# Attention plus mixture of experts on one core: the last stage unrolled, with twelve pairs of gathered rows, eight sums and eight residual rows in flight

## What is computed

```python
xn = layernorm(x)                                  # x: 2 x 2048 x 512, float32
out = x + attn(xn) + ffn(xn)
# attn: 16 heads of 32, latent keys and values of 128, causal softmax; out projection Wo, bias bo
# ffn: 8 experts, the two with the highest gate logit of each token
all_out = relu(einsum('nsd,edo->nseo', x, expert_w) + expert_b)
ffn = take_along_axis(all_out, top_idx).mean(axis=2)
```

## Time and profile before

| What | Value |
|---|---|
| Median of 3 timed runs | 1820.98 us |
| The profiled execution's own time | 1818.49 us |
| Its span, from the first to the last instruction | 1816.8 us |
| PE busy | 1619.3 us (89%) |
| DVE, ACT, POOL busy | 1207.6, 987.9, 583.0 us |
| Mean granted clock of TensorE, as a share of full speed | 0.963 |

### The profile page before, as it was taken

One profiled execution on the slowest core, in us unless ns is written; L12 is line 12 of the kernel. 1 busy time (PEld: TensorE's weight loads), 2 busy tenths in 40 slices (PEclk: granted clock), 3 DMA queues, 4 the chain that ended last, 5 costly groups with the idle time before them and its releaser, 6 DMA issues.

```text
span 1816.8 us, 46170 instructions
## 1 busy us (share of the span) xinstructions
PE 1619.3 (89%) x13286; PEld 919.7 (51%) x13287; DVE 1207.6 (66%) x2682; ACT 987.9 (54%) x1884; POOL 583.0 (32%) x972
## 2 busy tenths in 40 slices
PE   4676675988999999999999999999999899998776
PEld 2566662444555555555555555555555355554332
DVE  3888877556777777777777777777777244444555
ACT  2556661555666666666666666666666533333332
POOL 1456652566212112112112112211211333332554
PEclk8898996999999999999999999999999899999999
DMA  5486764011001001001001001101100155555776
GB/s 142 136 248 197 239 186 114 21 29 24 24 24 47 23 23 47 23 23 47 24 23 42 28 23 37 33 23 31 39 23 24 47 173 173 173 173 151 229 233 220
DMA packets 126985, 160.87 MB, mean 89 GB/s; under 512 B 28352, under 2 KB 77504, under 8 KB 126816
## 3 DMA queue, kind: packets, MB, share of 16 engines
q1 hardware_dynamic: 108336, 121.15, 21.9%
q0 software_dynamic: 12992, 35.77, 7.2%
q10 hardware_dynamic: 5616, 3.45, 0.6%
HBM read 99.03 MB, written 61.15 MB: 88 GB/s over the span
## 4 chain that ended last, share of the span: by engine, by line
PE 73%; DVE 10%; DMA 5%; issue 5%; ACT 4%; POOL 1%; ACTq 1%; DVEq 0%; SPq 0%; another core or an unknown queue 0%; POOLq 0%
PE PS L1209 28%; PE PS L1156 26%; PE PS L1259 10%; DMA arena<-expert_rows,cur 4%; PE PS L1221 3%; DVE pm L967 3%; PE PS L1242 2%; ACT arena L671 1%; ACT arena L683 1%; PE PS L1127 1%; DVE arena L1030 1%; PE PS L1104 1%; DVE arena L841 1%; PE PS L1110 1%; DMA eb_bc<-in_expert_b 1%
## 5 line engine op out<-in xcount | busy, mean ns | idle before, releaser
L967 DVE TENSOR_REDUCE pm<-PS 128x1 f32<-128x512 f32 (+3 forms) x1280 | 731.5, 602 | 301.9 <-PE PS L1156 287.9
L712 ACT ACTIVATE arena<-PS 128x512 f32<-128x512 f32 (+1 forms) x1152 | 607.9, 575 | 281.2 <-PE PS L1156 266.8
L1156 PE MATMUL PS<-arena 96*64 96x512 f16 (+7 forms) x5120 | 726.1, 355 | 38.0 <-DVE pm L967 20.2
L1209 PE MATMUL PS<-arena 128*33 128x512 f32 (+3 forms) x2560 | 661.9, 534 | 1.0 <-POOL arena L541 1.0
L1156 PEld LDWEIGHTS PS<-arena 96*64 96x64 f16 (+1 forms) x5120 | 353.2, 110 | 369.3 <-issue 143.3
L541 POOL TENSOR_SCALAR_AFFINE_SELECT arena<-arena 128x256 f32<-128x256 f32 (+1 forms) x256 | 110.9, 433 | 406.7 <-ACT arena L712 403.3
L1209 PEld LDWEIGHTS PS<-arena 128*33 128x33 f32 x2560 | 172.8, 112 | 85.4 <-POOL arena L541 3.6
L1156 PE MATMUL PS<-later,deny 128*64 128x128 f16 x1024 | 173.6, 222 | 0.0
L1259 PE MATMUL PS<-w_hi,arena 128*128 x576 | 172.1, 381 | 0.3 <-issue 0.3
L729 ACT ACTIVATE arena<-PS 128x1024 f16<-128x1024 f32 x72 | 73.8, 1024 | 150.5 <-PE PS L1242 145.1
L1007 DVE SCALAR_TENSOR_TENSOR arena<-PS,eb_bc 128x512 f32<-128x512 f32 x72 | 49.8, 691 | 127.0 <-PE PS L1259 127.0
(11 more groups left out here) (172 smaller groups left out, 1643.5 us busy)
## 6 DMA issues: line engine op xcount, KB each, us to landing
expert_rows<-arena SPq DMA_DIRECT2D x72, 256.0 KB, 2.0
arena<-q_pieces SPq DMA_DIRECT2D x96, 128.0 KB
arena<-k_pieces SPq DMA_DIRECT2D x96, 128.0 KB
v_rows<-arena SPq DMA_DIRECT2D x8, 1056.0 KB, 7.0
arena<-v_rows SPq DMA_DIRECT2D x32, 264.0 KB
arena<-in_x SPq DMA_DIRECT2D x8, 1024.0 KB, 7.1
xn_rows<-arena SPq DMA_DIRECT2D x16, 512.0 KB, 4.6
arena<-in_expert_w SPq DMA_DIRECT2D x32, 256.0 KB, 4.0
```

Source lines behind the costliest of these rows:

```text
L712: a.activation(probs[kk % 4][:, a_ * CH:a_ * CH + w], PS[:, s2_bank(k, x), 0:w], ACT.Exp, scale=SCALE).then_inc(s["exp_done"], 1)
L967: v.reduce_max(pm[:, c, r, p:p + 1], PS[:, S1_BANK[n], 0:w], AX).then_inc(s["s1_done"], 1)
L1156: last = t.matmul(PS[h:h + P // 2, bank, cols], lhsT[:, h:h + P // 2], rhs, start=start, stop=stop)
L1209: last = t.matmul(PS[rows_, 6 + c % 2, CH - wds[a]:CH], v_sb[pu % 2][:, j + a, :], probs[pk % 4][:, a * off:a * off + wds[a]], start=p_ in ...
```

## The change

- The two buffers each of gathered pairs, sums and residual rows become rings of 12, 8 and 8. The gathered rows and the sums lie where `w_hi` and `w_lo` were; the experts' last matmul has read them before POOL passes its wait for all 72 stores. The residual rows take the room in arena2, and `x_g`'s three further buffers have their own places there.
- Every buffer of the rings has a semaphore of its own, which starts at zero.
- SP waits for `norm_done` after the attention stage and loads the first eight residual rows before it stores the first tile of the experts. In the last stage it stores the sum of tile n and then loads the residual row of tile n + 8.
- POOL no longer copies indices to `cur`: each gather reads its column of `place` directly. It waits for the sum of tile n - 12 from tile 12 on.
- DVE waits for the store of tile n - 8, PE for the first instruction of the sum of tile n - 2 (the one that reads PSUM) in place of its last.
- On all engines the stage's loop over pairs is written out: 32 tiles, with constants in place of register values. The order of the operations on ACT, DVE and PE is as before.

```diff
-        xc = [tD(E) for _ in range(B)]
...
-        acc = [tD(E) for _ in range(B)]
-        y_g = [[tD(E) for _ in range(TOP)] for _ in range(B)]
-        x_g = [x_g0[:, :]] + [y_g[q // 2][q % 2].bitcast(f16) for q in range(1, AHEAD_G)]
+        x_ahead = [tD(E).bitcast(f16) for _ in range(AHEAD_G - 1)]
+        xc = [tD(E) for _ in range(8)]
+        spare = [w[:, :, :].rearrange("p e f -> p (e f)").bitcast(f32)[:, q * E:(q + 1) * E]
+                 for w in (w_hi, w_lo) for q in range(NE * KB * E // (2 * E))]
+        y_g, acc = [spare[TOP * q:TOP * (q + 1)] for q in range(12)], spare[TOP * 12:]
+        x_g = [x_g0[:, :]] + x_ahead
...
@@ SyncE @@
+            sp.wait_ge(s["norm_done"], count(NC * BH))
+            for n in range(len(xc)):
+                residual(n)
             with sp.Fori(0, PT // 2) as i:
                 for u in range(2):
                     sp.wait_ge(s["y_done"], count(i * 2 + u + 1))
                     sp.dma_start(y_dram[ds((i * 2 + u) * P, P), :], y_sb[u]).then_inc(s[f"y_st{u}"], 16)
-            for u in range(B):
-                residual(0, u)
-            with sp.Fori(0, ST - 1) as i:
-                for u in range(B):
-                    result(i, u)
-                    residual(i + 1, u)
...
+            for n in range(NT):
+                result(n)
+                if n + len(xc) < NT:
+                    residual(n + len(xc))
...
@@ GpSimd @@
-            with pool.Fori(0, ST) as i:
-                for u in range(B):
-                    n = i * B + u
-                    pool.wait_ge(s["acc_done"], count(n - 1))
-                    g.tensor_copy(cur[:, TOP * u:TOP * (u + 1)],
-                                  place[:, :, ds(i + u * ST, 1)].rearrange("p k o -> p (k o)")).then_inc(s["cur_done"], 1)
-                    pool.wait_ge(s["cur_done"], count(PT + n + 1))
-                    pool.sem_inc(s["gather_at"], 1)
-                    for k in range(TOP):
-                        g.indirect_dma_start(out=y_g[u][k], out_offset=None, in_=y_dram,
-                                             in_offset=bass.IndirectOffsetOnAxis(ap=cur[:, TOP * u + k:TOP * u + k + 1], axis=0)
-                                             ).then_inc(s[f"yg_in{u}"], 16)
+            for n in range(NT):
+                q, at = n % len(y_g), n // B + n % B * ST
+                if n >= len(y_g):
+                    pool.wait_ge(s["acc_done"], count(n - len(y_g) + 1))
+                for k in range(TOP):
+                    g.indirect_dma_start(out=y_g[q][k], out_offset=None, in_=y_dram,
+                                         in_offset=bass.IndirectOffsetOnAxis(ap=place[:, k, at:at + 1], axis=0)
+                                         ).then_inc(s[f"yg_in{q}"], 16)
...
@@ VectorE @@
-                dve.wait_ge(s[f"out_done{u}"], count(i * 16))
-                dve.wait_ge(s[f"xc_in{u}"], count((i + 1) * 16))
+                if n >= len(acc):
+                    dve.wait_ge(s[f"out_done{r}"], n // len(acc) * 16)
+                dve.wait_ge(s[f"xc_in{x_}"], (n // len(xc) + 1) * 16)
                 dve.wait_ge(s["proj_ps"], count(n + 1))
...
-                dve.wait_ge(s[f"yg_in{u}"], (i + 1) * (16 * TOP))
...
+                dve.wait_ge(s[f"yg_in{y_}"], (n // len(y_g) + 1) * (16 * TOP))
...
@@ TensorE @@
-                    pe.wait_ge(s["acc_done"], count(n - 1))
+                if n >= B:
+                    pe.wait_ge(s["dveE"], count((n - B) * 2 + 1))
```

More of the change, by code:

```diff
@@ L214, in layer_kernel @@
         START = 4
[L215 to L216 removed]
+        FROM_ZERO = ["id_zero", "id_done", "ids_in", "xg_in0", "xg_in1", "xg_in2", "xg_in3"] + OUT_SEMS
         def count(n):
@@ L444, in _ @@
                     sp.dma_start(y_dram[ds((i * 2 + u) * P, P), :], y_sb[u]).then_inc(s[f"y_st{u}"], 16)
[L446 to L451, removed]
-            for u in range(B):
-                residual(0, u)
-            with sp.Fori(0, ST - 1) as i:
-                for u in range(B):
-                    result(i, u)
-                    residual(i + 1, u)
-            for u in range(B):
-                result(ST - 1, u)
-            for w in range(B):
-                sp.wait_ge(s[f"out_done{w}"], count(16 * ST))
+            for n in range(NT):
+                result(n)
+                if n + len(xc) < NT:
+                    residual(n + len(xc))
+            for q in range(len(acc)):
+                sp.wait_ge(s[f"out_done{q}"], 16 * len(range(q, NT, len(acc))))
         @block.gpsimd
@@ L748, in turned_heads @@
                              PS[:, 4 + 2 * u:6 + 2 * u, :].rearrange("p z c -> p (z c)"), ACT.Copy).then_inc(s["oT_done"], 1)
-            for u in range(B):
-                first_piece(0, u)
-            with act.Fori(0, ST - 1) as i:
-                for u in range(B):
-                    turned_heads(i * B + u, u)
-                    first_piece(i + 1, u)
-            for u in range(B):
-                turned_heads((ST - 1) * B + u, u)
+            for n in range(B):
+                first_piece(n)
+            for n in range(NT):
+                turned_heads(n)
+                if n + B < NT:
+                    first_piece(n + B)
         @block.vector
@@ L1027, in sums @@
                 dve.wait_ge(s["proj_ps"], count(n + 1))
-                lnk(v.scalar_tensor_tensor(out=acc[u], in0=PS[:, u, :], scalar=1.0 / WS, in1=xc[u], op0=ALU.mult, op1=ALU.add))
-                dve.wait_ge(s[f"yg_in{u}"], (i + 1) * (16 * TOP))
-                lnk(v.tensor_tensor(acc[u], acc[u], y_g[u][0], ALU.add))
-                v.tensor_tensor(acc[u], acc[u], y_g[u][1], ALU.add).then_inc(s["acc_done"], 1)
-            for u in range(B):
-                second_piece(0, u)
-            with dve.Fori(0, ST - 1) as i:
-                for u in range(B):
-                    second_piece(i + 1, u)
-                    sums(i, u)
@@ L1039, in _ @@
-            for u in range(B):
-                sums(ST - 1, u)
+                lnk(v.scalar_tensor_tensor(out=acc[r], in0=PS[:, u, :], scalar=1.0 / WS, in1=xc[x_], op0=ALU.mult, op1=ALU.add))
+                dve.wait_ge(s[f"yg_in{y_}"], (n // len(y_g) + 1) * (16 * TOP))
+                lnk(v.tensor_tensor(acc[r], acc[r], y_g[y_][0], ALU.add))
+                v.tensor_tensor(acc[r], acc[r], y_g[y_][1], ALU.add).then_inc(s["acc_done"], 1)
+            for n in range(B):
+                second_piece(n)
@@ L1043, in _ @@
+            for n in range(NT):
+                if n + B < NT:
+                    second_piece(n + B)
+                sums(n)
         @block.tensor
@@ L1280, in turn_heads @@
                 last.then_inc(s["otp_ps"], 1)
-            def outs(i, more):
-                for u in range(B):
-                    n = i * B + u
-                    if u == 0 or more:
-                        turn_heads(n + 1, 1 - u)
-                    pe.wait_ge(s["oT_done"], count(n + 1))
-                    pe.wait_ge(s["acc_done"], count(n - 1))
-                    terms = [(k, z, y) for k in range(KB) for z, y in pairs]
-                    for q_, (k, z, y) in enumerate(terms):
-                        last = t.matmul(PS[:, u, :], oT[u][:, z, k, :], comb_hl[:, y, k, :],
-                                        start=q_ == 0, stop=q_ == len(terms) - 1)
-                    last.then_inc(s["proj_ps"], 1)
-            turn_heads(0, 0)
-            with pe.Fori(0, ST - 1) as i:
-                outs(i, True)
-            outs(ST - 1, False)
+            turn_heads(0, 0)
+            for n in range(NT):
+                u = n % B
+                if n + 1 < NT:
+                    turn_heads(n + 1, 1 - u)
+                pe.wait_ge(s["oT_done"], count(n + 1))
+                if n >= B:
+                    pe.wait_ge(s["dveE"], count((n - B) * 2 + 1))
+                terms = [(k, z, y) for k in range(KB) for z, y in pairs]
+                for q_, (k, z, y) in enumerate(terms):
+                    last = t.matmul(PS[:, u, :], oT[u][:, z, k, :], comb_hl[:, y, k, :],
+                                    start=q_ == 0, stop=q_ == len(terms) - 1)
+                last.then_inc(s["proj_ps"], 1)
 _INS = ["x", "Wq", "Wdkv", "Wuk", "Wuv", "ln_g", "ln_b", "Wo_h", "Wo", "bo", "gate_w", "gate_b", "expert_w", "expert_b"]
```

32 lines of the change are left out of this document (19 added, 13 removed).

## The result

The changed kernel took 1810.34 us (median of 6 runs, 1803.05 to 1812.82) beside 1819.78 us for the kernel before (6 runs). The ratio is 0.9942, with a 95% interval of 0.9921 to 0.9962: faster by 0.58%, 9.4 us, where 42.7 us were forecast. The profiled execution's span is 1808.4 us, 8.4 less than before.

The account below looks back on a forecast made before the run. The prediction took the last stage to be bound by a chain of waits for gathered rows, 9.18 us a pair of tiles. Terms -45.2 + 1.5 + 1.0 = -42.7 us from 1820.98 gave 1778.3, rounded to 1778.0; range 1772 to 1790.

Parts of the forecast that it names:

- At no cost: Last stage: PE's earlier wait, semaphores, constants and written-out code cost nothing; the range holds 9.6 us for POOL's gaps.
- POOL's port: Rival, last stage: gathers beside DVE's two-input instructions take 1.62 us each, 4.8 us more, 1783 in all; chance 0.18.
- PE's pace: Last stage: with rows ready, the loop of PE and DVE sets 3.06 us a tile, where a tile took 4.59.
- The late first rows: Start of the last stage: the first tile's sum waits for its gathered rows, 1.6 us once.
- The gathers: Last stage: POOL's two gathers per tile take 2.92 us, just under PE's 3.06; late landings are charged 1.5 us.
- The sign that I had named: Last stage, if right: gathers 1.25 to 1.6 us apart up to tile 12, then held by the sum.
- The last stage as a whole: Last stage: 45.2 us gained by the faster pace, less 1.5 us for late landings of gathered rows.
- The residual rows at the start: Start of the expert stage: eight residual loads delay the first awaited gathers by 1.0 us, bounds 0 and 6.0.
- The sum: Whole kernel: -45.2 + 1.5 + 1.0 = -42.7 us.
- DMA as a bound: Rival, last stage: transfers need 3.34 us a tile, more than PE's 3.06, so 1781 to 1791 us; chance 0.22.
- the share at 1.0 that I had named as its sign: Last stage: DMA share at 1.0, waits for residual or gathered rows throughout and landings over 5 us would show DMA bounding.
- The full exclusion of gathers and two-input instructions: Rival, last stage: gathers and DVE's two-input instructions take turns, 4.69 us a tile against 4.59, 1825 in all; chance 0.03.

Follow-up runs that it names:

- the later runs: The changed kernel, unedited, timed again on four occasions on three chips beside the kernel before: 37 to 44 us gained.
- changed_again: The changed kernel without an edit, run once more beside the kernel before: ratio 0.9777.
- loops8: The changed kernel with the last stage's loops back on ACT, PE and DVE and 8 gathered pairs instead of 12: 1758.09 us beside 1797.87, ratio 0.9785.
- lead4: The changed kernel with POOL waiting for the sum of tile n - 4 instead of n - 12: 1757.20 us beside 1797.87, ratio 0.9783.
- rings2: The changed kernel with rings of two; written-out code, removed index copy and PE's earlier wait stay: 1778.64 us beside 1797.87, ratio 0.9891.

## Why the prediction was wrong, and where it was right

**What failed in the measured case.** The step that failed is "At no cost", which put semaphores and written-out code at nothing, with a range that held 9.6 us for what the rows had no price for. It took for granted that a signal of PE reaches ACT and DVE at once beside a stream of gathers. The rival "POOL's port" looked for the gathers' disturbance in DVE's port only. In the first measurement PE's signals came up to 29 us late, and the last stage took 31 us more for it (137.4 against 106.6 us). That the rest of the sum holds in the later runs leaves this step as the one that made the forecast miss. The kernel before had a trace of it that I didn't read: from 330 to 450 us, where PE did 817 matmuls, it has waits of DVE and ACT marked "issue" and "remote". I had looked only at the stages that the change touches.

**What held.** Set against the later runs, where the conditions of that measurement are absent, the working comes out term by term, with one term too small:
- PE's pace. Forecast 3.06 us a tile. In `changed_again`, from PE's turn at 1652.30 (tile 2) to 1742.93 (tile 31) are 29 steps of 3.125 us on the average, with the early delays in it.
- The late first rows. Forecast 1.6 us once. Measured there: four short waits for rows at the start, 1.8 us in all, and PE's waits for L1014 of 3.4 us in three (2.4 of them stand before the stage's first turn in both kernels).
- The gathers. Forecast 1.25 to 1.62 us each, 1.46 taken. Measured 1649.03 to 1734.8 for 63 steps: 1.36. Landings were later than I took, 5.3 us in the median (3.2 to 6.9) instead of 3.85, but after the first tiles they are covered. POOL never waited for a sum, so the ring of twelve never filled. The sign that I had named, gathers held by the sum from tile 12 on, didn't come, and four pairs are enough.
- The last stage as a whole. Forecast 45.2 - 1.5 = 43.7 us shorter. Measured 151.0 us from PE's first turn in the profile before (1816.8 - 1665.8) and 106.6 in `changed_again`, 44.4 shorter. A profile of the kernel before in the later conditions isn't on record; its last stage has none of the waits in question.
- The residual rows at the start. Forecast 1.0 us, between 0 and 6.0. Measured 12.61 - 9.09 = 3.5 us (3.1 in the first measurement). This term was too small by 2.5 us: I argued that different queues share at once. In `changed_again` PE starts on the two first gathers 5.9 and 7.1 us after their issue (1413.77 to 1419.66, 1415.86 to 1422.98), where 3.6 us were before:

```profile
1415.86 0.98 POOL L594 DMA_INDIRECT arena<-xn_rows,cur_id  x1 [0.84 <-POOL cur_id L591]
...
1422.98 1.03 PE L1236 MATMUL PS<-ident,arena 128*128 128x128 f16 x8 [2.30 <-DMA arena<-xn_rows,cur_id]
```

- The sum. -42.7 us forecast; -41.1, -37.5, -44.0 and -40.2 us on the four occasions.

**The rivals.** DMA as a bound: its share is 1.00 in `changed_again` at 362 GB/s and PE still has no wait for it, so the share at 1.0 that I had named as its sign isn't one. The overlap of packets that the earlier trace rows showed fits this. The full exclusion of gathers and two-input instructions, at the price that I gave it, didn't come: in the stretch from 1653.79 to 1664.95 the gathers take 0.96 to 1.29 us beside DVE. But they do take turns, for a short part of the gather. Two pairs of rows show the two cases:

```profile
1700.71 0.76 DVE L1026 TENSOR_TENSOR w_lo<-w_lo,w_hi 128x512 f32<-128x512 f32 x1
1700.74 0.96 POOL L609 DMA_INDIRECT w_hi<-expert_rows,place  x1 [0.30 <-issue]
...
1704.47 0.69 DVE L1027 TENSOR_TENSOR w_lo<-w_lo,w_hi 128x512 f32<-128x512 f32 x1
1704.58 1.41 POOL L609 DMA_INDIRECT w_lo<-expert_rows,place  x1 [0.30 <-issue]
```

Of the 64 gathers of this stage 33 take 0.95 us. Each of the other 31 ends 0.82 to 0.83 us after the end of an instruction of DVE with two SBUF operands that was under way, as the one at 1704.58 does (1705.99 against 1705.17). The Trainium skill's rule (SBUF — State Buffer, "Who interferes with whom") that the second to issue is blocked until the first has finished fits these rows, which cost POOL up to 0.47 us each. In six other cases, like the one at 1700.74, the gather began 0.03 to 0.04 us after DVE's instruction and was not held; there DVE's took 0.76 or 0.77 us in place of 0.69, which the rule doesn't foretell. No instruction of DVE waited for a whole gather. So where I priced a turn at the whole gather, the rows show it at a small part of it. The prediction read the earlier trace rows as speaking against a full block; the row there fits the same pattern, since the gather ends at 1705.44, 0.86 us after the first of the two instructions beside it.

**What the traces say of the cause, and what stays open.** Two causes were in question for the stalls of the first measurement. Theory F, PE's signals reach the others late, has the recorded times for it: three signals 14 to 29 us late in the last stage, 65 and 55 late ones from 330 to 450 us, none in the later profiles. It also fits that PE's turn at 1689.40 follows DVE's L1014 at once. Theory A, code is loaded late, has the traces against it. Transfers of code have queues of their own in the profile, marked `instruction`. The first profile has none under way from 1687.9 to 1741.5 us, so none arrived just before the two engines went on. The queues that moved anything from 1690 to 1715 us are these two (packets, MB, share of 16 engines):

```profile
q0 software_dynamic: 1503, 4.90, 65.4%
q1 hardware_dynamic: 287, 0.52, 6.1%
```

And the first profile isn't short of such transfers: it holds 61 in all, as `changed_again` does. What stays open is why PE's signals came late, and why in those conditions only. The late signals go with a stream of indirect DMAs from POOL, in two stretches of the one profile and one of the other; the last signals came 1.9 us after the queue had run empty, at 1713.4 us, but ACT had got an earlier one at 1694.98 with the queue full. The kernels that would vary the stream there, `loops8` and `lead4`, never met the conditions, so whether fewer tiles ahead shorten the stall isn't known. One more rival is untested. In those conditions the record is itself thinner: it holds 11434 updates by DMAs in the changed kernel's first profile and 13773 in `changed_again`. Something that holds back records and signals alike, the recording itself included, isn't excluded.

## What to carry to other kernels

When a buffer ring is widened, ask which ring is next: more gathered pairs alone gave 7 us, and residual rows and sums another 14. Four tiles ahead did what twelve did, and what was taken out of the circle itself (the copy in front of the gathers, with the other edits that `rings2` keeps) gave as much as all the rings. A result that misses a well-worked sum by 30 us is worth one more run of the same kernel, on another chip if there is one, before any theory of the kernel is built on it. And where two engines go on at the same instant, the recorded times of the semaphores that they wait for tell late work from a late signal.

## What the hardware showed that I had not expected

- The same two kernels differ by 0.6% in one measurement and by 2.1 to 2.5% in four later ones, through idle times of up to 26 us in ACT and DVE while POOL issues indirect DMAs every 1.27 us. PE's signals for them are recorded 14 to 29 us after its matmuls.
- A gather issued by POOL beside DVE's two-input instructions took 0.95 us or, when one was under way, ended 0.83 us after it; DVE's instruction grew from 0.69 to 0.77 us at the most.
- Eight loads of 256 KB on SP's queue, issued in 3.8 us, delayed gathers on the software queue: PE could start on them 5.9 and 7.1 us after their issue in place of 3.5 and 3.6. A queue of its own didn't protect them.
- DMA at a share of 1.00 and 362 GB/s over 40 us left PE full; the stage's first three gathers landed in 3.2 to 3.5 us, the median of all 64 was 5.3 us.
